# One block of attention: the order of projections, scores and products of 64-wide heads

## The reference

```python
def _L2_xattn_ref(x, context, ln_gamma, ln_beta, w_q, w_kv, w_out, b_out, gate):
    # 16 heads, 64 wide, INNER = 1024
    xn = _layernorm(x, ln_gamma, ln_beta)
    q = (xn @ w_q).reshape(B, SQ, NUM_HEADS, DIM_HEAD)
    kv = context @ w_kv
    k, v = jnp.split(kv, 2, axis=-1)
    ...
    scores = jnp.einsum('bqhd,bkhd->bhqk', q * SCALE, k)
    attn = jax.nn.softmax(scores, axis=-1)
    out = jnp.einsum('bhqk,bkhd->bqhd', attn, v).reshape(B, SQ, INNER)
    out = out @ w_out + b_out
    return out * jnp.tanh(gate[0])
```

## Time and profile before

| | us |
|---|---|
| median of 3 runs | 3267.42 (3264.63 to 3269.26) |
| span of the profiled execution | 3275.2 |
| stage L2x: first to last matmul group | 1028.97 to 1926.4 |
| of it from the first T to the last T | 1064.13 to 1910.63 |
| PE busy over the whole span | 2790.8 (85%) |
| DVE, ACT, POOL busy over the whole span | 1837.6, 1281.2, 914.8 |

### The profile page before, as it was taken

One profiled execution on the slowest core, in us unless ns is written; L12 is line 12 of the kernel. 1 busy time (PEld: TensorE's weight loads), 2 busy tenths in 40 slices (PEclk: granted clock), 3 DMA queues, 4 the chain that ended last, 5 costly groups with the idle time before them and its releaser, 6 DMA issues. The chain is left out here.

```text
span 3275.2 us, 49624 instructions
## 1 busy us (share of the span) xinstructions
PE 2790.8 (85%) x18594; PEld 1943.4 (59%) x18594; DVE 1837.6 (56%) x4118; ACT 1281.2 (39%) x2502; POOL 914.8 (28%) x755
## 2 busy tenths in 40 slices
PE   2999994978876999999999956479999627999998
PEld 1566652657664666666666635345555426888887
DVE  4777765865935555555555548767777432222222
ACT  1444446853571433333333348524445301111111
POOL 0555551001300211111111112335555262222222
PEclk8999997989988999999999979889999758999999
DMA  6766631010001000000000000086764421333322
GB/s 137 136 118 117 118 64 39 1 58 1 1 6 60 7 7 4 8 4 7 4 4 7 1 29 1 26 154 123 122 122 84 121 85 39 69 96 67 70 63 36
DMA packets 155697, 181.67 MB, mean 55 GB/s; under 512 B 24128, under 2 KB 132960, under 8 KB 155488
## 3 DMA queue, kind: packets, MB, share of 16 engines
q1 hardware_dynamic: 132256, 145.13, 21.5%
q0 software_dynamic: 14496, 20.36, 3.4%
q10 hardware_dynamic: 8736, 13.37, 1.3%
HBM read 129.10 MB, written 49.71 MB: 55 GB/s over the span
## 5 line engine op out<-in xcount | busy, mean ns | idle before, releaser
L907 POOL TENSOR_TENSOR L2x_halves_sum<-L2x_probs 128x512 f32<-128x512 f32 x128 | 163.1, 1274 | 848.0 <-ACT L2x_probs L921 848.0
L2000 PE MATMUL L3f_pH<-L3f_xgT,L3f_W 128*128 128x256 f32 x1184 | 265.2, 382 | 8.9 <-ACT L3f_hT L2029 8.2
L2008 PE MATMUL L3f_pY<-L3f_W,L3f_hT 128*128 128x256 f32 x1184 | 261.7, 379 | 0.0
L2000 PEld LDWEIGHTS L3f_pH<-L3f_xgT,L3f_W 128*128 128x128 f32 x1184 | 225.8, 191 | 42.5 <-ACT L3f_hT L2029 10.6
L2008 PEld LDWEIGHTS L3f_pY<-L3f_W,L3f_hT 128*128 128x128 f32 x1184 | 222.1, 190 | 28.7
L3226 ACT ACTIVATE L0x_probs<-L0x_pT 128x512 f32<-128x512 f32 x256 | 151.3, 600 | 215.3 <-PE L0x_pT L3491 213.2
L3226 ACT ACTIVATE L3x_probs<-L3x_pT 128x512 f32<-128x512 f32 x256 | 152.3, 597 | 201.7 <-PE L3x_pT L3491 198.9
L3349 DVE TENSOR_REDUCE L0x_mx<-L0x_pS 128x2 f32<-128x512 f32 x256 | 168.8, 687 | 110.6 <-PE L0x_pS L3475 110.1
L2029 ACT ACTIVATE L3f_hT<-L3f_pH,L3f_b 128x256 f32<-128x256 f32 x148 | 69.4, 473 | 411.0 <-PE L3f_pH L2000 347.7
L3349 DVE TENSOR_REDUCE L3x_mx<-L3x_pS 128x2 f32<-128x512 f32 x256 | 167.4, 686 | 98.7 <-PE L3x_pS L3475 98.2
L3203 POOL TENSOR_TENSOR L3x_halves<-L3x_probs 128x512 f32<-128x512 f32 x128 | 168.2, 1318 | 190.7 <-ACT L3x_probs L3226 190.7
(11 more groups left out here) (585 smaller groups left out, 6276.2 us busy)
## 6 DMA issues: line engine op xcount, KB each, us to landing
L0x_k_stack<-L0x_k_parts_dram SPq DMA_DIRECT2D x128, 128.0 KB, 4.9
L3x_k_stack<-L3x_k_parts_dram SPq DMA_DIRECT2D x128, 128.0 KB, 4.8
L0x_q_stack<-L0x_q_parts_dram SPq DMA_DIRECT2D x32, 384.0 KB, 9.3
L3x_q_stack<-L3x_q_parts_dram SPq DMA_DIRECT2D x32, 384.0 KB, 9.2
L3f_W<-in_L3f_W ACTq DMA_DIRECT2D x12, 1024.0 KB
L3f_xg<-tokens_by_expert SPq DMA_DIRECT2D x38, 260.0 KB
L0x_k_parts_dram<-L0x_k_parts SPq DMA_DIRECT2D x16, 384.0 KB, 2.8
L0x_q_parts_dram<-L0x_q_parts SPq DMA_DIRECT2D x16, 384.0 KB, 2.7
```

Source lines behind the costliest of these rows:

```text
L907: nc.gpsimd.tensor_tensor(halves_sum[n % 2][:, :, :], probs[n % 2][:, :, 0, :], probs[n % 2][:, :, 1, :], ALU.add).then_inc(halved, 1)
L2000: ins = nc.tensor.matmul(pH[c % 4][:, 0:TILE], W1[par][:, kc, c * P:(c + 1) * P], xgT[:, kc, :], start=kc == 0, stop=kc == KC - 1)
L2008: ins = nc.tensor.matmul(pY[j][:, 0:D], hT[:, c, j * P:(j + 1) * P], W2[par][:, c, :], start=c == 0, stop=c == HCH - 1)
```

## The change

Two unused functions go (`attention` and `staggered`, called by nothing; they are left out below). In `wide_attention` the order of every engine's stream is written anew:

- the fills of a slot stand together behind T, K and Q of the same pairs side by side, and the four V in two slots;
- each slot has one S (`scores_at`), directly ahead of T. It is of pair `p + 1` of the next batch; slot 7's is pair 0 of the batch after that;
- P of the pair before stands first in the slot, so that the order is P, S, T, fills, where it was T, (S), fill, P, (S), fill;
- K, Q and `xnT` are of batch `r + 2` in slots 4 to 7 and 3; V stays at `r + 1`, output at `r - 1`;
- `inverse` and `divide` run one slot behind T and no longer two. `take_q` and `take_k` wait, from batch 1 on, until the bf16 copies that they overwrite have been read by S.

```diff
@@ -797,22 +156,24 @@
     CH = DI // P
     NPAIR = H // 2
 
-    FIRST = {0: ("k0",), 1: ("k1",), 2: ("k2",), 3: ("k3",), 4: ("out0",), 5: ("out1",), 6: ("v00",), 7: ("v10",)}
-    SECOND = {0: ("q0",), 1: ("q1",), 2: ("q2",), 3: ("q3",), 6: ("v01", "mT"), 7: ("v11", "xnT")}
-    S_FIRST = {2: 1, 3: 3, 4: 5, 5: 7}
-    S_SECOND = {1: 0, 2: 2, 3: 4, 4: 6}
-
-    def batch_of(name, r):
-        return r - 1 if name[:3] == "out" else r + 2 if name == "xnT" else r + 1
-
-    def fills_of(r, table, p):
-
-        return [(name, batch_of(name, r)) for name in table.get(p, ()) if 0 <= batch_of(name, r) < B]
+    FILLS = {0: ("v00", "v01"), 1: ("v10", "v11"), 2: ("out0",), 3: ("out1", "xnT"),
+             4: ("k0", "q0"), 5: ("k1", "q1"), 6: ("k2", "q2"), 7: ("k3", "q3", "mT")}
+    AHEAD = {"v": 1, "o": -1, "x": 2, "k": 2, "q": 2, "m": 1}
+
+    def fills_of(r, p):
+
+        named = [(name, r + AHEAD[name[0]]) for name in FILLS[p]]
+        return [(name, b) for name, b in named if 0 <= b < B]
+
+    def scores_at(r, p):
+
+        b, pair = (r + 2, 0) if p == NPAIR - 1 else (r + 1, p + 1)
+        return [(b, pair)] if 0 <= b < B else []
 
     place = {}
     for r in range(-2, B + 1):
         for p in range(NPAIR):
-            for fill in fills_of(r, FIRST, p) + fills_of(r, SECOND, p):
+            for fill in fills_of(r, p):
                 place[fill] = (len(place) % 2, len(place) // 2)
 
     with ExitStack() as ctx:
@@ -929,8 +290,8 @@
 
             def take_q(b, m):
                 src, taken = filled(act, f"q{m}", b)
-                if b and m == 0:
-                    act.wait_ge(s_ready, NPAIR * b)
+                if b:
+                    act.wait_ge(s_ready, NPAIR * (b - 1) + 2 * m + 2)
                 src = src[:, :].rearrange("p (c s) -> p c s", c=2)
                 nc.scalar.activation(qT[b % 2][:, 2 * m:2 * m + 2, :], src, ACT.Copy)
                 nc.scalar.activation(q_b[:, 2 * m:2 * m + 2, :], src, ACT.Copy).then_inc(taken, 1)
@@ -949,16 +310,17 @@
 
             for r in range(-2, B + 1):
                 for p in range(NPAIR):
-                    back = NPAIR * r + p - 2
+                    if p == 0 and 0 <= r < B:
+                        take_mT(r)
+                    if p == 4 and 0 <= r + 2 < B:
+                        take_xnT(r + 2)
+                    if p == 0 and 0 <= r + 1 < B:
+                        take_q(r + 1, 3)
+                    if 5 <= p and 0 <= r + 2 < B:
+                        take_q(r + 2, p - 5)
+                    back = NPAIR * r + p - 1
                     if 0 <= back < NPAIR * B:
                         inverse(back // NPAIR, back % NPAIR)
-                    if 0 <= r + 1 < B:
-                        if p == 0:
-                            take_xnT(r + 1)
-                        if 1 <= p <= 4:
-                            take_q(r + 1, p - 1)
-                        if p == 7:
-                            take_mT(r + 1)
                     if 0 <= r < B:
                         exp(r, 2 * p)
                         exp(r, 2 * p + 1)
@@ -983,6 +345,8 @@
 
             def take_k(b, m):
                 src, taken = filled(dve, f"k{m}", b)
+                if b:
+                    dve.wait_ge(s_ready, NPAIR * (b - 1) + 2 * m + 2)
                 src = src[:, :].rearrange("p (c s) -> p c s", c=2)
                 nc.vector.tensor_copy(kT[b % 2][:, 2 * m:2 * m + 2, :], src)
                 nc.vector.tensor_copy(kT_b[:, 2 * m:2 * m + 2, :], src).then_inc(taken, 1)
@@ -1037,28 +401,28 @@
                 dve.wait_ge(x_new, TB * b + j + 1)
                 nc.vector.bn_stats(core.stats[:, TB * b + j, :], x_t)
 
+            normalize(0)
             for r in range(-2, B + 1):
                 for p in range(NPAIR):
-                    back = NPAIR * r + p - 2
+                    if p in (1, 2) and 0 <= r + 1 < B:
+                        take_v(r + 1, p - 1, 0)
+                        take_v(r + 1, p - 1, 1)
+                    if p in (3, 4) and 0 <= r - 1 < B:
+                        residual(r - 1, p - 3)
+                    for b, pair in scores_at(r, p):
+                        if pair == 0 and b:
+                            split_max(b - 1)
+                            dve.wait_ge(m_lo, b)
+                        maximum(b, pair)
+                    if r == B - 2 and p == NPAIR - 1:
+                        split_max(B - 1)
+                    back = NPAIR * r + p - 1
                     if 0 <= back < NPAIR * B:
                         divide(back // NPAIR, back % NPAIR)
-                    if 0 <= r + 1 < B:
-                        if p in S_FIRST:
-                            maximum(r + 1, S_FIRST[p])
-                        if p < 4:
-                            take_k(r + 1, p)
-                        if p == 6:
-                            split_max(r + 1)
-                    if p in (4, 5) and 0 <= r - 1:
-                        residual(r - 1, p - 4)
-                    if 0 <= r + 1 < B:
-                        if p in S_SECOND:
-                            maximum(r + 1, S_SECOND[p])
-                        if p >= 6:
-                            take_v(r + 1, p - 6, 0)
-                            take_v(r + 1, p - 6, 1)
-                    if p == 6 and r + 2 < B:
-                        normalize(r + 2)
+                    if 4 <= p and 0 <= r + 2 < B:
+                        take_k(r + 2, p - 4)
+                    if p == 5 and 0 <= r + 3 < B:
+                        normalize(r + 3)
 
         @block.tensor
         def _(pe):
@@ -1166,18 +530,14 @@
             pe.wait_ge(setup, 1)
             for r in range(-2, B + 1):
                 for p in range(NPAIR):
-                    if 0 <= r < B:
-                        score_T_pair(r, p)
-                    if p in S_FIRST and 0 <= r + 1 < B:
-                        score_pair(r + 1, S_FIRST[p])
-                    for name, b in fills_of(r, FIRST, p):
-                        fill(name, b)
                     back = NPAIR * r + p - 1
                     if 0 <= back < NPAIR * B:
                         times_v_pair(back // NPAIR, back % NPAIR)
-                    if p in S_SECOND and 0 <= r + 1 < B:
-                        score_pair(r + 1, S_SECOND[p])
-                    for name, b in fills_of(r, SECOND, p):
+                    for b, pair in scores_at(r, p):
+                        score_pair(b, pair)
+                    if 0 <= r < B:
+                        score_T_pair(r, p)
+                    for name, b in fills_of(r, p):
                         fill(name, b)
 
 
```

More of the change, by code:

```diff
@@ L3539, in _ @@
                             fill(name, b)
-def staggered(eng, n, round_):
-    def flags(k):
-        return {d: 0 <= k + d < n for d in range(-2, 4)}
-    for k in range(3):
-        round_(k, k % 2, k // 2, flags(k))
-    pairs = (n - 6) // 2
-    with eng.Fori(0, pairs) as i:
-        round_(2 * i + 3, 1, i + 1, dict.fromkeys(range(-2, 4), True))
-        round_(2 * i + 4, 0, i + 2, dict.fromkeys(range(-2, 4), True))
-    for k in range(2 * pairs + 3, n):
-        round_(k, k % 2, k // 2, flags(k))
 def flat(ap):
```

548 lines of the change are left out of this document (removed).

## The result

The changed kernel takes 3244.47 us, median of 4 runs (3242.03 to 3249.23), against 3268.28 (3264.63 to 3269.26) for the kernel before, measured beside it: ratio 0.9932 [0.9918, 0.9946]. That is 23.8 us less, where the prediction said 11.0. The direction and the mechanism held; the size did not.

A forecast was written before the change was run, and what follows sets the result against it. TensorE's own instruction stream was taken as the bound. The start's +12.3 us and the body's -23.3 us gave -11.0 us, taken off the 3267.42 us median for a forecast of 3256.4 us, range 3249 to 3268.

The forecast's parts named there:

- K and Q joined, V joined: Fill runs in each round: joining two runs into one saves 0.79 us for K and Q, 0.39 us for V.
- S beside T: In each slot, S directly ahead of T costs 0.23 us and T 1.28; 0.24 us saved a round.
- (d): Slot 5's S no longer waits for the maximum on VectorE: 0.46 us saved a round.
- The wait that goes: The wait of slot 5's S on VectorE's maximum disappears, 0.46 us a round.
- The slots without fills: Rounds 0, 14 and 15: P waits for exponentials and GpSimd, so a slot costs 4.46 us, or 4.69 with S, not 2.73.
- The start: From xnT to the first T: two batches of keys and queries come first, so T starts 12.3 us later.
- After the last T: The part of the stage behind the last T was forecast to stay unchanged.
- The clock in the thin slots: Rival: the granted clock falls to 0.5 in slots without fills, 24 us more, result 3280 us; chance 0.12.
- The wait of mT: Rival: in slot 7 mT waits for take_k(3), 0.5 us a round, 7.5 us, result 3264; chance 0.08.
- The join without effect: Rival: Q still waits on its bank's semaphore between K and Q; 16.5 us lost, result 3273; chance 0.04.
- The dearer start: Rival: two more low-clock stretches of dense fills at the start, 3.4 us, result 3260 us; chance 0.08.

The follow-up runs named there:

- the split: The changed kernel with the first fill of slots 0, 1, 4, 5 and 6 put directly behind P, undoing 72 joins: 3261.05 us, ratio 0.9978.
- the joins alone: The kernel before with both fills of a slot together behind P, S in its old place, keys and queries one round ahead: 3252.98 us, ratio 0.9947.

## Why the prediction was right in kind and too small

**The bound** was TensorE's own stream, and stayed so: each edit moved the stage by what the start-to-start distances on TensorE said, waits included.

**K and Q joined, V joined:** forecast 3.65 and 3.63, measured 3.651 and 3.631. Confirmed by the split (+0.20 each) and by the joins alone.

**S beside T: the step that failed.** The prediction took 0.23 for S, which was right, and then said "A T after S then costs its 1.28 (T after P and T after a fill cost the same 1.28)". It measured 1.18. I had T's cost with P or a fill ahead of it, and never with S. But the rows were there: in the earlier trace rows the first four rows of T behind P or a fill print 0.70, and in the earlier trace rows those of the T at 1421.59, behind an S, print 0.60. The prediction's own decomposition, 0.20 for leaving a fill run and 0.10 for leaving T or S, has only costs of leaving. There is one of entering as well, about 0.10, that T pays and S in front of it takes away. S itself hardly pays it: it takes 0.315 behind T and 0.322 behind P, each with a fill behind. The term: 8 x 0.105 = 0.84 us a round, which is 53.41 less 52.57; over the 118 T with an S ahead it is 12.4 us, against the body's 12.3. The rest of the round was right, with one shift inside it: of the eight T of a round in the kernel before, one stood behind an S already, the one of the earlier trace rows, and by these prices it takes 1.08 of the 1.64 us and the wait in (d) 0.56, not 0.46. Seven T and the wait give the same 0.84. The kernel with T ahead of S and mT moved confirmed the term from the other end.

Where the 0.10 lies, the weight loads show. These rows are T's load behind S in the changed kernel and behind P in the kernel with T ahead of S, then the first matmul of a K behind T and of a Q behind K, in the changed kernel again.

```profile
1416.17 0.30 PEld L504 LDWEIGHTS L2x_pT<-L2x_qT,L2x_kT 64*128 64x128 f32 x4
...
1443.05 0.30 PEld L504 LDWEIGHTS L2x_pT<-L2x_qT,L2x_kT 64*128 64x128 f32 x4 [0.39 <-issue]
...
1417.46 0.48 PE L454 MATMUL L2x_pM<-L2x_ctxT,L2x_wk 128*128 128x256 f32 x1
...
1419.29 0.38 PE L454 MATMUL L2x_pM<-L2x_xnT,L2x_wq 128*128 128x256 f32 x1
```

Behind S, T's load starts 0.11 us ahead of T's first matmul (1416.28), under S; behind P it starts with it (1443.06). The same holds for every group whose shape differs from the one ahead: the load starts with the first matmul, and that matmul holds TensorE longer than the next ones. The longer the load, the more: by 0.01 us for S (load 0.09), 0.05 for P (0.13), 0.10 for T (0.18) and 0.10 for K (0.19), whose first two starts are 0.320 us apart and all later ones 0.216. So the prediction's 0.20 for leaving a fill run is two costs of about 0.10 as well, one of them paid on entering. For the joins that made no difference, since a join removes one entering and one leaving; for T it was the miss.

The Trainium skill ("TensorEngine Tiling (Array Packing)", Key Properties) says that a change of the tiling mode drains TensorE. The traces agree that changes cost (0.20 us a join), but their number alone does not set the time: the changed kernel and the one with T ahead of S have the same 24 a round, and their T with S differ by 0.094 us.

**The wait that goes:** S no longer waits in the round, as forecast; its size is above.

**The slots without fills:** 4.46 as forecast; 4.59 instead of 4.69 with an S, for the same reason as above. **The start:** 47.8 against 47.5; S behind S 2.14 against 2.1, and a low clock behind the thin stretch 1.4 us against 1.6. **After the last T:** unchanged, 15.76 us in both.

**The rivals.** *The clock in the thin slots* fell: 1.00 at 9.67 of 14.00 us busy. The Trainium skill ("TensorE: Matmul & The Clock Gate", Why this matters for your kernels) warns of idle gaps between bursts; gaps of 1.18 and 0.26 us a slot didn't lower the clock here. The gaps that it means are longer than these, so it doesn't give this rival, as the prediction had it. The start's thin stretch with 1.75 and 0.88 was followed by the low level. *The wait of mT* did not come in the changed kernel, but its place and slack were right: 0.24 us, and moving S by 1.19 us made it 0.757. *The join without effect* fell. *The dearer start* came to 0.3 us.

**The range** ended at 3249: below the forecast it allowed for the clock at the start and for roundings, and for no gain left out. The bound below should have asked what T costs behind each possible neighbour.

**What stays open.** That the length of the load sets the price of entering is read from four groups that differ in shape and operation too; no run changes the type alone. In round 14 the kernel with P behind the next T has two waits that were not removed: P of slot 5 waits 0.63 us for the exponentials, and batch 15's first T 0.47 us for ScalarE's copy of mT.

## To carry to other kernels

Price a group of matmuls by the distance from its start to the next start, for each pair of neighbours ahead and behind that the new order will have; a short bf16 group of the same shape can take away a cost of entering from a float32 one. When work is moved ahead by a round, check what slots it empties, and let the consumer lag by enough to cover them. Put groups that wait for a round trip to another engine between long fills, at the start too.

## What was not expected of the hardware

- A 64-row float32 group of 12 rows costs 1.180 us start to start behind a 64-row bf16 group and 1.285 behind any 128-row one, both with a fill run or P behind it; with S behind it and a 128-row group ahead, 1.188. So entering and leaving cost about 0.10 each, and a second 128x128 float32 run costs 0.20 for both (3.651 for one run of sixteen rows, 3.85 for two of eight).
- The bf16 group of 4 rows pays 0.09 for leaving and under 0.01 for entering.
- The granted clock stayed at 1.00 (the 2.4 GHz level) through slots 69% busy (9.67 of 14.00 us) with idle pieces of 1.2 us. Behind the start's stretch at 43% (1.97 of 4.60 us), with pieces up to 1.75 us, it was 0.50, and K took 3.38 us as printed instead of 1.99.
- A thin stretch is not always followed by the low level. In the kernel with the joins alone TensorE was busy 1.19 of 4.15 us ahead of the first V (1055.00 to 1059.15), with two pieces of 1.48, and the clock stayed at 1.00 through it and behind it. With T ahead of S, the same start as in the changed kernel was followed by a low level through K and Q both (3.78 and 2.96 us printed, against 3.38 and 1.89). So the 1.4 us of clock at the start can differ from one kernel to the next.
